# Gated context of a cross-attention kernel: VectorE reads the context's bank itself, and ScalarE's four scaled copies go

## Reference

```python
memory_proj = einsum('bme,de->bmd', memory, W_mem)
scores = einsum('bnd,bmd->bnm', hidden_states, memory_proj) / sqrt(D)
attn = softmax(scores, axis=-1)
memory_context = einsum('bnm,bmd->bnd', attn, memory_proj)
gate_input = concatenate([hidden_states, memory_context], axis=-1)
gate = sigmoid(einsum('bnf,df->bnd', gate_input, W_gate) + b_gate)
fused = hidden_states + gate * memory_context
out = fused * rsqrt(mean(square(fused), -1) + 1e-6) * norm_w
```

## Time and profile before

| | |
|---|---|
| median of 3 runs | 562.02 us (561.62 to 562.85) |
| span of the profiled execution | 560.6 us |
| PE busy | 541.7 us, 97% |
| DVE busy | 503.4 us, 90% |
| ACT busy | 336.2 us, 60% |
| POOL busy | 134.1 us, 24% |
| `copy_ctx` on ACT (line 696) | 32 of 678 ns |
| `gate_ctx` on DVE (line 984) | 32 of 788 ns on average |
| `add_x` on DVE (line 991) | 32 of 948 ns on average |

### The profile page before, as it was taken

The page is one execution under the profiler, slowest core; times in us unless marked ns, Lnnn a source line. Parts: engine busy times, 40 slices in busy tenths (PEclk is TensorE's granted clock), DMA queues, the critical chain, the costliest instruction groups (busy, mean ns, idle before and its releaser), DMA issues.

```text
span 560.6 us, 9004 instructions
## 1 busy us (share of the span) xinstructions
PE 541.7 (97%) x2432; PEld 438.8 (78%) x2432; DVE 503.4 (90%) x847; ACT 336.2 (60%) x633; POOL 134.1 (24%) x102
## 2 busy tenths in 40 slices
PE   8999999999999999999999999999999999999992
PEld 7777888878887788878888788887888778887871
DVE  4879959999899998899998998999988999889966
ACT  4676646665567646576366665666565864667534
POOL 0005600244003520055001440025300451005600
PEclk9999999999999999999999999999999999999988
DMA  9965371520683117711385115841088212100033
GB/s 226 260 127 83 90 132 50 98 73 18 148 176 97 37 50 136 167 68 37 98 163 104 56 37 134 171 114 40 0 170 177 75 37 99 52 23 20 0 114 112
DMA packets 184338, 54.25 MB, mean 97 GB/s; under 512 B 161528, under 2 KB 174848, under 8 KB 184320
## 3 DMA queue, kind: packets, MB, share of 16 engines
q1 hardware_dynamic: 183792, 53.52, 40.9%
q10 hardware_dynamic: 528, 0.52, 0.3%
HBM read 45.63 MB, written 8.39 MB: 96 GB/s over the span
## 4 chain that ended last, share of the span: by engine, by line
PE 66%; DVE 17%; issue 10%; SPq 3%; ACT 2%; DMA 2%; ACTq 0%; DVEq 0%
PE bank L357 14%; PE bank L358 13%; PE bank L359 13%; PE bank L524 7%; PE bank L525 7%; PE bank L526 7%; DVE p_lo L838 5%; DVE s L879 3%; DVE fused L984 2%; DVE fused L991 2%; DVE gate L905 2%; ACT fused L696 2%; DVE gate L934 2%; DMA fused<-in_L_xattn_W_gate_dram 2%; SPq L249 2%
## 5 line engine op out<-in xcount | busy, mean ns | idle before, releaser
L1155 POOL TENSOR_TENSOR psum_rows<-psum_rows,p_tmp 128x512 f32<-128x512 f32 (+1 forms) x88 | 122.5, 1392 | 85.4 <-ACT p_tmp L673 84.3
L838 DVE TENSOR_TENSOR p_lo<-p_tmp,p_hi 128x512 fp32r<-128x512 f32 (+1 forms) x104 | 92.3, 889 | 5.5 <-ACT p_hi L635 5.4
L673 ACT ACTIVATE p_tmp<-s 128x512 f32<-128x512 f32 (+1 forms) x104 | 65.2, 628 | 45.1 <-DVE s L879 44.5
L1155 POOL TENSOR_TENSOR psum_rows<-p_tmp 128x512 f32<-128x512 f32 x8 | 10.8, 1354 | 309.4 <-ACT p_tmp L673 309.4
L357 PE MATMUL bank<-q_hi,mt_hi 128*128 128x512 f32 (+1 forms) x208 | 81.7, 393 | 0.0
L358 PE MATMUL bank<-q_lo,mt_hi 128*128 128x512 f32 (+1 forms) x208 | 81.2, 390 | 0.0
L359 PE MATMUL bank<-q_hi,mt_lo 128*128 128x512 f32 (+1 forms) x208 | 81.1, 390 | 0.0
L525 PE MATMUL bank<-p_lo,mem_hi 128*128 128x512 f32 (+1 forms) x208 | 81.0, 389 | 0.0
L524 PE MATMUL bank<-p_hi,mem_hi 128*128 128x512 f32 (+1 forms) x208 | 81.0, 389 | 0.0
L526 PE MATMUL bank<-p_hi,mem_lo 128*128 128x512 f32 (+1 forms) x208 | 80.9, 389 | 0.0
L635 ACT ACTIVATE s<-bank 128x512 f32<-128x512 f32 (+1 forms) x104 | 62.0, 597 | 19.5 <-PE bank L359 19.1
(11 more groups left out here) (93 smaller groups left out, 1057.6 us busy)
## 6 DMA issues: line engine op xcount, KB each, us to landing
mem_raw<-in_ctx_dram SPq DMA_DIRECT2D x48, 256.0 KB, 3.0
mem_blocks<-in_ctx_dram SPq DMA_DIRECT2D x64, 136.0 KB
x_again<-in_x_dram SPq DMA_DIRECT2D x32, 256.0 KB, 2.6
out_dram<-fused SPq DMA_DIRECT2D x32, 256.0 KB, 2.1
x_raw<-in_x_dram SPq DMA_DIRECT2D x112, 64.0 KB, 2.1
mem_blocks<-in_ctx_dram SPq DMA_DIRECT2D x56, 64.0 KB, 2.0
x_raw<-in_x_dram SPq DMA_DIRECT2D x4, 256.0 KB, 4.7
gate<-in_L_xattn_W_gate_dram SPq DMA_DIRECT2D x2, 512.0 KB, 6.1
```

Of the source, the lines that this page charges most:

```text
L673: nc.scalar.activation(p_tmp[0:r, t % TMP_RING, :], s[0:r, t, :], ACT.Exp, scale=float(D) ** -0.5).then_inc(exp_done, 1)
L838: return nc.vector.tensor_tensor(dst, src, hi.bitcast(F32), ALU.subtract)
L1155: nc.gpsimd.tensor_tensor(psum_rows[0:r, :], a, p_tmp[0:r, t % TMP_RING, :], ALU.add).then_inc(p_added, 1)
```

## The change

The four copies of each batch are dropped. `gate_ctx(j)` takes the context from its bank (one SBUF tile, one bank) and writes (1 + tanh) x context into `fused`; it waits for PE's product and for the store of the previous output. `add_x(j)` becomes a multiply-add: `fused` x `r_half` + x. The semaphore `ctx_copied` goes; PE's `context(j)` for j = 2 and 3, and DVE's first transpose of the next x, wait for `gated` (counted by `gate_ctx`) instead. `add_x` waits for `r_done` too.

```diff
--- before.py
+++ after.py
@@ -174,7 +174,7 @@
         s_copied, mt_has_hi, mem_has_hi = sem("s_copied"), sem("mt_has_hi"), sem("mem_has_hi")
         exp_done, p_has_hi, xt_has_hi = sem("exp_done"), sem("p_has_hi"), sem("xt_has_hi")
         q_has_hi, u_has_hi = sem("q_has_hi"), sem("u_has_hi")
-        ctx_copied, tanh_done, squares_done = sem("ctx_copied"), sem("tanh_done"), sem("squares_done")
+        tanh_done, squares_done = sem("tanh_done"), sem("squares_done")
 
         xt_done, mt_done = sem("xt_done"), sem("mt_done")
         run_done, mt_has_lo, mem_has_lo = sem("run_done"), sem("mt_has_lo"), sem("mem_has_lo")
@@ -487,7 +487,7 @@
 
                 if j >= 2:
 
-                    pe.wait_ge(ctx_copied, NT * b + j - 1)
+                    pe.wait_ge(gated, NT * b + j - 1)
                 n = slice(j * P, (j + 1) * P)
                 product(bank[CTX_BANK + j % 2][:, :], [
                     (u_hi[:, c, n], u_lo[:, c, n], wt_hi[:, c, :], wt_lo[:, c, :]) for c in range(CT)
@@ -685,16 +685,6 @@
                     exp(b, t, first)
                 if t >= 1:
                     p_hi_part(b, t - 1)
-
-            def copy_ctx(b, j):
-
-                act.wait_ge(pe_ctx, NT * b + j + 1)
-                if j == 0:
-                    act.wait_ge(r_done, b + 1)
-
-                act.wait_ge(fused_free[j], 16 * (b + 1))
-                nc.scalar.activation(fused[:, j, :], bank[CTX_BANK + j % 2][:, :], ACT.Copy,
-                                     scale=r_half[:, j : j + 1]).then_inc(ctx_copied, 1)
 
             def tanh(b, j):
 
@@ -775,14 +765,11 @@
                             q_hi_part(b + 1, 1)
                 else:
                     tanh(b - 1, 0)
-                    copy_ctx(b - 1, 0)
                     tanh(b - 1, 1)
                     for t in range(MT + 1):
                         for q in SPLIT_BY_SOFTMAX.get(t, []):
                             mem_hi_part(b, q, first)
                         softmax(b, t, first)
-                        if t in (0, 2, 3):
-                            copy_ctx(b - 1, max(t, 1))
                         if t in (2, 3):
                             tanh(b - 1, t)
                         if t == 1:
@@ -819,7 +806,6 @@
             iteration(B - 1, False, True)
             for j in range(NT):
                 tanh(B - 1, j)
-                copy_ctx(B - 1, j)
                 if j >= 1:
                     squares(B - 1, j - 1)
             squares(B - 1, NT - 1)
@@ -969,7 +955,7 @@
                             dve.wait_ge(wt_split_lo, 8)
                         else:
 
-                            dve.wait_ge(ctx_copied, NT * b)
+                            dve.wait_ge(gated, NT * b)
                     transpose_x(b + 1, X_BLOCKS_AT.index(t))
                 if t in MEM_BLOCKS_AT:
                     if t == MEM_BLOCKS_AT[0] and not first:
@@ -980,16 +966,19 @@
             def gate_ctx(b, j):
 
                 dve.wait_ge(tanh_done, NT * b + j + 1)
-                dve.wait_ge(ctx_copied, NT * b + j + 1)
-                nc.vector.scalar_tensor_tensor(fused[:, j, :], gate[:, j, :], 1.0, fused[:, j, :],
+                dve.wait_ge(pe_ctx, NT * b + j + 1)
+
+                dve.wait_ge(fused_free[j], 16 * (b + 1))
+                nc.vector.scalar_tensor_tensor(fused[:, j, :], gate[:, j, :], 1.0, bank[CTX_BANK + j % 2][:, :],
                                                ALU.add, ALU.mult).then_inc(gated, 1)
 
             def add_x(b, j):
 
                 dve.wait_ge(gated, NT * b + j + 1)
                 dve.wait_ge(in_x_again[j % 2], 16 * (2 * b + j // 2 + 1))
-                nc.vector.tensor_tensor(fused[:, j, :], fused[:, j, :], x_again[:, j % 2, :],
-                                        ALU.add).then_inc(fused_done, 1)
+                dve.wait_ge(r_done, b + 1)
+                nc.vector.scalar_tensor_tensor(fused[:, j, :], fused[:, j, :], r_half[:, j : j + 1],
+                                               x_again[:, j % 2, :], ALU.mult, ALU.add).then_inc(fused_done, 1)
 
             def rms(b):
```

## The result

The changed kernel takes 556.74 us (median of 6 runs, 555.79 to 557.10) against 561.79 us (6 runs, 560.55 to 562.85): the recorded ratio is 0.990, 95% interval 0.9885 to 0.992, and the two medians give 0.991. That is 5.05 us less, about 0.9%; forecast were 3.8.

What follows compares the result with a forecast made beforehand. PE was taken as bound, waiting in batches only for DVE's add_bias. Six batches x 0.50 = 3.0, last batch 0.9, tail -0.1: 3.8 us, 562.0 - 3.8 = 558.2 us; own range 556.3 to 560.3, 8-in-10 range 554.5 to 562.8.

Steps and rivals of the forecast that it cites:

- What bounds the kernel: PE is busy nearly all the time; inside batches it waits for DVE's add_bias, before gate_x(2) and gate_x(3).
- The bound of 1.32 us a pass: Most a faster vector engine can bring at PE's gate_x gaps: 1.32 us in each of seven batches, 9.2 in all.
- Step 1: DVE's gate_ctx(0) can begin about 0.6 us earlier, but gate_input(1) waits for PE's product and leads by only 0.10.
- Steps 3 and 4: On DVE gate_ctx(1) leads by 0.36 us; on ACT exp(1) leads by 0.54, so POOL's first addition starts at 238.61.
- Steps 5 and 6: The lead passes through POOL's additions to DVE; gate_x(2)'s gap closes, add_bias(1) leads by 0.50 us a batch.
- The wait that was to be left: PE waits for add_bias once a batch, 0.53 us before gate_x(3), in all 3.7 us instead of 5.9.
- Step 2: On DVE each add_x costs 0.06 us more as multiply-add (bounds 0 and 0.55); gate_ctx from the bank keeps 0.69.
- doubled-`add_x` rival: Each add_x on DVE takes 0.55 us more, 1.0 us a batch slower: about 571 us; chance 0.04.
- Steps 7 and 8: Lead kept to the next batch, 1.9 us slack before context(3); last batch gains 0.9 us, tail loses 0.1.
- the larger gain: Rival: add_x(2) goes ahead of POOL's addition and loses its wait, 1.0 us a batch: 554.7 us; chance 0.13.
- one more operation meet POOL: Rival: another two-SBUF-tile DVE operation waits for POOL, losing 0.2 to 0.4 us a batch: 563.4 to 564.8 us; chance 0.07.
- No change: Rival: exp(1) does not move up and p_lo(0) ends as before: 562.0 us within 0.2%; chance 0.18.

Runs made afterwards that it cites:

- either of two other means: Changed kernel with POOL's additions cut to 8 of 512 columns, 550.46 us; or with add_x(2) moved behind add_bias(1), 550.34 us.
- The idle copies: Changed kernel with idle ACT copies put back each pass: one between exp(0) and exp(1), 559.84 us; or three at the other copies' places, 556.18 us.
- the moved copy: Kernel before with copy_ctx(1) moved ahead of exp(0) on ACT, nothing dropped: 559.66 us, ratio 0.9965.
- the longer wait: Changed kernel with two idle 128x512 reductions on DVE ahead of the last pass's u_lo: 558.47 us, ratio 0.9934.

## Why the prediction came out

It held by its own chain, with one term too small; the measured time lies near the lower end of the forecast's own range, 556.3 to 560.3 us.

- *What bounds the kernel*: right. With the gaps closed by either of two other means a pass is 64.54 us. The bound of 1.32 us a pass was too low by 0.16, of which 0.11 is the delay that the wait before `gate_x(3)` also puts on the matmul after the first.
- *Step 1* (0.10 for `gate_input(1)`, the rest a wait for PE): the trace shows it to 0.01 us.
- *Steps 3 and 4* (`gate_ctx(1)` at 238.30; `exp(1)` ahead by 0.54, POOL's addition at 238.61): 238.30 and 238.54 in the old count. The idle copies and the moved copy show that `exp(1)` carries the gain.
- *Steps 5 and 6, the term of 0.50 us a pass*: the mechanism was right, the size is 0.67 (4.01 us in six passes instead of 3.0). `exp(1)` follows `exp(0)` at once, 0.07 earlier than the distance to its shift made it; POOL's first addition takes 1.30 instead of 1.36 us; and the lead of 0.54 need not have been rounded down to 0.50, since the 0.06 us of `add_x(1)` and `(2)` vanish in their waits for POOL: 0.54 + 0.07 + 0.06 = 0.67.
- *The wait that was to be left* (3.7 us in all, 0.53 a pass): measured are 3.4 and 0.50. That it came so close is luck. With the lead of 0.66 by which `gate_x(3)` starts earlier, and the 0.34 of the prediction, it would be 0.37; but `gate_x(2)` ends 0.47 earlier and not 0.34, since its first matmul no longer delays the next: 0.69 - 0.66 + 0.47 = 0.50.
- *Step 2* (0.06 us for each `add_x`): right as a duration (0.74 us), charged too often. The "0.18 already counted" of the doubled-`add_x` rival doesn't fit the prediction's own chain either, which takes off only some 0.04 of it. The rule of the Trainium skill ("Vector Engine (DVE) Microarchitecture Reference", "Points that are easy to get wrong") stays contradicted for this form: the group of the new `add_x` has a median of 752 ns with the waits for POOL in it, and a mean of 737 ns with POOL's additions cut.
- *Steps 7 and 8*: no wait of PE for `gate_ctx`; the gap before the tail closed (0.44 us, and 0.51 for the last pass: 0.95 against the 0.90 forecast); the tail 0.08 longer, forecast 0.1. That the gap also closes with the idle copy back in its place fits the prediction's reason for it, the wait of `gate_ctx(3)` that is gone; by itself this was not tried.
- *The rivals*: of the larger gain nothing came; `add_x(2)` still waits, 1.49 us. Nor did one more operation meet POOL. "No change" is excluded by the interval, "slower" with it.
- The sum by the traces is 4.9 us; the medians differ by 5.05.

## What to carry to other kernels

Where two engines hold each other through a third, ask of an edit not how much work it takes off an engine but what stood ahead of the instruction that the third one waits for. Here one copy of four carried nearly all of the gain in a pass (0.59 of 0.67 us), and swapping two operations in a queue gave half of it (0.32). An operation that is long because it waits should be moved out of the stretch that the bounding engine waits for: changing one number (`add_x(2)` two steps later) gave more than the whole change, and it shares the gap with it, so such gains must not be added up.

## What the runs showed of the hardware that was not expected

- A VectorE operation with two SBUF tiles that meets a POOL addition ends about 0.5 us after it, and an extra cost of its own form (0.06 us for the column) does not show in such a wait: 1.12 us with the column and 1.13 without.
- TensorE drops from 2.4 to 1.2 GHz for about 3.4 us in the tail in some runs only. In the profile before, it had done the eight one-column matmuls of `row_sums` and stood idle for 0.40 us up to 537.52; the matmuls take 0.63 us each from 538.67 on instead of 0.39, and the mean clock from 537 to 543 us is 0.72. The traces of two other kernels disagree: with the copy moved (wait 0.37 us) the granted clock is 0.76 from 537 to 543 us, with `add_x` alone (wait 0.41 us) it is 1.00. Of 51 runs of that kernel 16 have a mean granted clock of 0.992 or less, with a median of 562.8 us against 561.3 for the others. Where that idle time is 0.41, 0.37 and 1.16 us (the runs with `add_x` alone, with the copy moved, with the longer wait), 2 of 12, 5 of 12 and 3 of 6 runs have such a clock. In the kernels whose wait there is under 0.15 us it was 1 of 39 (one run of the changed kernel, at 556.2 us, so its time shows no cost). So about 0.5 us of the 5.05 can be this, on average (1.5 us in 16 of 51 runs). That the short wait is the cause is not shown, and what decides in which runs the stage comes stays open.
